# Layer-normalisation scaling moved from VectorE to GpSimd, and a residual sum cut in four, in an attention kernel

## What is computed

```python
x = x + 0.5 * ffn(layernorm(x))
x = x + attn(layernorm(x))
x = x + 0.5 * ffn(layernorm(x))
```

## Time and profile before

| | us |
|---|---|
| median of 3 executions | 3069.32 |
| lowest and highest | 3068.89, 3074.65 |
| the profiled execution, its own time | 3079.44 |
| its span, first to last instruction | 3077.6 |
| mean granted TensorE clock | 0.973 |

### The profile page before, as it was taken

The page is one execution under the profiler, slowest core; times in us unless marked ns, Lnnn a source line. Parts: engine busy times, 40 slices in busy tenths (PEclk is TensorE's granted clock), DMA queues, the critical chain, the costliest instruction groups (busy, mean ns, idle before and its releaser), DMA issues.

```text
span 3077.6 us, 96889 instructions
## 1 busy us (share of the span) xinstructions
PE 2752.8 (89%) x36160; PEld 1078.5 (35%) x36160; DVE 2810.2 (91%) x5659; ACT 2737.8 (89%) x5028; POOL 899.5 (29%) x1195
## 2 busy tenths in 40 slices
PE   5989998989989899898998988988988888898887
PEld 2323443434434334343343433333323333232323
DVE  4999999999999999999999998999999999899986
ACT  2999888988889888898888989898998989899897
POOL 3333213322133221332313332122332312233222
PEclk8999999999999999999999999999999999999999
DMA  8222342323423234232341323433223343322332
GB/s 221 53 48 60 57 98 40 68 49 56 98 38 63 55 56 98 37 62 57 56 98 36 61 59 70 85 70 63 50 59 69 70 85 64 67 48 61 72 70 56
DMA packets 155355, 206.63 MB, mean 67 GB/s; under 512 B 34530, under 2 KB 88290, under 8 KB 154723
## 3 DMA queue, kind: packets, MB, share of 16 engines
q1 hardware_dynamic: 154594, 199.37, 31.3%
q0 software_dynamic: 256, 0.52, 0.1%
HBM read 46.66 MB, written 25.17 MB: 23 GB/s over the span
## 4 chain that ended last, share of the span: by engine, by line
PE 36%; issue 20%; SPq 18%; DVE 11%; POOL 8%; ACT 4%; DMA 2%; DVEq 0%; POOLq 0%; ACTq 0%
SPq L374 18%; PE ring L833 12%; PE ring L770 11%; PE o_acc L847 10%; DVE exp_ring L656 9%; POOL kq_parts L365 2%; POOL kq_rest L361 2%; POOL kq_parts L363 2%; POOL kq_parts L359 2%; PE ring L892 1%; ACT exp_ring L580 1%; DMA kq_stack<-kq_parts 1%; POOL v_scaled L513 1%; ACT w_xn L592 1%; PE ring L869 1%
## 5 line engine op out<-in xcount | busy, mean ns | idle before, releaser
L580 ACT ACTIVATE exp_ring<-exp_ring,neg_max 128x1024 f32<-128x1024 f32 x2048 | 2344.7, 1146 | 271.3 <-DVE exp_ring L656 254.5
L656 DVE TENSOR_SCALAR_CACHE_REDUCE exp_ring<-ring 128x1024 f32<-128x1024 f32 x2048 | 2408.9, 1216 | 189.1 <-PE ring L833 184.5
L833 PE MATMUL ring<-kq_stack 128*32 128x512 bf16 x16384 | 1165.7, 387 | 201.2 <-DVE exp_ring L656 50.7
L847 PE MATMUL o_acc<-exp_ring,v_scaled 128*32 128x512 f32 x8224 | 1091.7, 607 | 59.1 <-POOL v_scaled L513 37.9
L833 PEld LDWEIGHTS ring<-kq_stack 128*32 128x32 bf16 x16384 | 401.9, 97 | 1147.2 <-issue 413.3
L513 POOL TENSOR_TENSOR v_scaled<-v_now,exp_rsums 128x64 f32<-128x64 f32 x513 | 155.2, 303 | 1790.1 <-DVE exp_rsums L671 1770.4
L580 ACT ACTIVATION_READ_ACCUMULATOR exp_ring<-exp_ring,neg_max 128x1 f32 x2048 | 381.9, 186 | 0.0
L847 PEld LDWEIGHTS o_acc<-exp_ring,v_scaled 128*32 128x32 f32 x8224 | 249.7, 112 | 293.8 <-POOL v_scaled L513 64.4
L770 PE MATMUL ring<-ffn_wo_wowff,o_T 128*32 128x256 f32 x4352 | 258.4, 380 | 4.2 <-DVE exp_ring L656 2.8
L770 PE MATMUL ring<-xn_T,ffn_wqkv 128*32 128x512 f32 x2112 | 257.8, 609 | 3.0 <-DVE exp_ring L656 1.9
L359 POOL TENSOR_TENSOR kq_parts<-kq_stage,zero 128x512 bf16<-128x512 f32 x130 | 143.0, 1100 | 225.7 <-ACT kq_stage L610 144.5
(11 more groups left out here) (102 smaller groups left out, 1283.0 us busy)
## 6 DMA issues: line engine op xcount, KB each, us to landing
kq_stack<-kq_parts SPq DMA_DIRECT2D x2072, 64.0 KB, 2.4
x_post<-x_slots SPq DMA_DIRECT2D x17, 1024.0 KB, 5.5
x_prep<-x_slots SPq DMA_DIRECT2D x16, 1024.0 KB, 8.3
x_slots<-x_post SPq DMA_DIRECT2D x8, 1024.0 KB, 6.1
out<-x_post SPq DMA_DIRECT2D x8, 1024.0 KB, 4.5
x_prep<-in_L_attn_x SPq DMA_DIRECT2D x1, 1024.0 KB, 6.0
exp_ring<-in_L_attn_w_qkv SPq DMA_DIRECT2D x1, 512.0 KB
kq_stack<-kq_parts POOLq DMA_DIRECT2D x8, 64.0 KB, 3.6
```

Of the source, the lines that this page charges most:

```text
L580: nc.scalar.activation(e, e, ACT.Exp, bias=negmax[:, i % NM:i % NM + 1], scale=-1.0, accum_out=sums[:, g % EG, c:c + 1]).then_inc(exp_done, 1)
L656: nc.vector.tensor_scalar(E[:, (g % EG) * HQ + c, :].rearrange("p (b n) -> p b n", b=NB), ps, -1.0, None, ALU.mult, ALU.min, accum_out=neg ...
L833: last = mm(ps[k:k + COLS, n, :], kq[:, 0, c, j * P + k:j * P + k + COLS], kq[:, 1, c, n * BANK:(n + 1) * BANK], start=True, stop=True)
L847: last = mm(O[32 * c:32 * c + 32, n, :], vsc[a][:, g % EG, c, :], E[:, (g % EG) * HQ + c, n * BANK:(n + 1) * BANK], start=(a == 0 and j == ...
```

## The change

Both normalisations' scaling goes from VectorE to GpSimd. On GpSimd it is a `tensor_scalar` with two operands, add and multiply, so the mean is negated first, once per normalisation, in a small operation behind the power. Ahead of the first call, and of any call that directly follows a split in GpSimd's order, stands a one-element addition into `pool_sink`. The places of `xn` and `xn2` stay. `x1` has four pieces of two token tiles, a tile apart, and the places of `ln2_stats` follow them. The waits on `x1_done` count to four.

```diff
+    X1 = 4
+    POOL_STEPS = ("ln_rstd", "ln2_rstd", "xn", "xn2", "qk", "recip", "u_norm", "w_norm", "xbias")
...
     PLAIN = {
-        "x1": (72.1, 72.2),
+        "x1": (72.1, 73.1, 74.1, 75.1),
...
     WITH_LINEAR = {
-        "x1": (36.1, 36.2),
-        "ln2_stats": (36.3, 36.7, 36.8, 36.8, 38.2, 38.4, 38.6, 39.1),
+        "x1": (35.1, 36.1, 37.1, 38.1),
+        "ln2_stats": (36.2, 37.2, 37.4, 38.2, 38.4, 39.2, 39.4, 40.1),
...
     SP:
-                    sp.wait_ge(x1_done, (p + 1) * 2)
+                    sp.wait_ge(x1_done, (p + 1) * X1)
                     sp.dma_start(tokens(out[p - LINEAR]), xr[:]).then_inc(out_stored, 16)
...
     GpSimd, in part():
+                    if kind in POOL_STEPS:
+                        after_split, prev = prev == "qk", kind
                     if kind == "ln_rstd":
                         pool.wait_ge(var_ready, p + 2)
                         nc.gpsimd.tensor_tensor(rstd[:], rstd[:], half_neg[:], ALU.pow).then_inc(rstd_ready, 1)
+                        nc.gpsimd.tensor_tensor(negm[:], zero[:, 0:1].to_broadcast([P, NT]), mv[:, :, 0],
+                                                ALU.subtract).then_inc(negm_ready, 1)
+                    elif kind == "xn":
+                        if i == 0:
+                            pool.wait_ge(negm_ready, p + 2)
+                            pool.wait_ge(rstd_ready, p + 2)
+                        if i == 0 or after_split:
+                            nc.gpsimd.tensor_tensor(psink[:], zero[:], zero[:], ALU.add)
+                        nc.gpsimd.tensor_scalar(xp[:, i, :], xp[:, i, :], negm[:, i:i + 1], rstd[:, i:i + 1],
+                                                ALU.add, ALU.mult).then_inc(xn_ready, 1)
...
+                    elif kind == "xn2":
+                        if i == 0:
+                            pool.wait_ge(negm2_ready, p + 1)
+                            pool.wait_ge(rstd2_ready, p + 1)
+                        if i == 0 or after_split:
+                            nc.gpsimd.tensor_tensor(psink[:], zero[:], zero[:], ALU.add)
+                        nc.gpsimd.tensor_scalar(wb[:, i, 0:D], xr[:, i, :], negm2[:, i:i + 1], rstd2[:, i:i + 1],
+                                                ALU.add, ALU.mult).then_inc(xn2_ready, 1)
...
     VectorE, in part():
-                        k = NT // 2
+                        k = NT // X1
...
-                    elif kind == "xn":
-                        dve.wait_ge(rstd_ready, p + 2)
-                        nc.vector.tensor_scalar(xp[:, i, :], xp[:, i, :], mv[:, i, 0:1], rstd[:, i:i + 1],
-                                                ALU.subtract, ALU.mult).then_inc(xn_ready, 1)
...
-                        dve.wait_ge(x1_done, p * 2 + i // 4 + 1)
+                        dve.wait_ge(x1_done, p * X1 + i // (NT // X1) + 1)
...
-                    elif kind == "xn2":
-                        dve.wait_ge(rstd2_ready, p + 1)
-                        nc.vector.tensor_scalar(wb[:, i, 0:D], xr[:, i, :], mv2[:, i, 0:1], rstd2[:, i:i + 1],
-                                                ALU.subtract, ALU.mult).then_inc(xn2_ready, 1)
```

More of the change, by code:

```diff
@@ L205, in build_macaron @@
         rstd2 = sb("rstd2", [P, NT])
+        negm = sb("neg_mean", [P, NT])
+        negm2 = sb("neg_mean2", [P, NT])
+        psink = sb("pool_sink", [P, 1])
         ssu = sb("sumsq_u", [P, NT])
@@ L273, in build_macaron @@
         xn2_ready = sem("xn2_ready")
+        negm_ready = sem("negm_ready")
+        negm2_ready = sem("negm2_ready")
         xt2_act = sem("xt2_act")
@@ L291, in build_macaron @@
                          y_dve: 4, xbias_done: 4, x_stored: 16, ln2_stats: NT, ln2_aggr: NT,
-                         var2_ready: 1, rstd2_ready: 1, xn2_ready: NT}
+                         var2_ready: 1, rstd2_ready: 1, xn2_ready: NT, negm2_ready: 1}
         START = 2
@@ L433, in phase @@
                 if isinstance(p, int):
-                    sp.wait_ge(x1_done, 2)
+                    sp.wait_ge(x1_done, X1)
                 elif not linear:
-                    sp.wait_ge(x1_done, (p + 1) * 2)
+                    sp.wait_ge(x1_done, (p + 1) * X1)
                     sp.dma_start(tokens(out[p - LINEAR]), xr[:]).then_inc(out_stored, 16)
@@ L453, in _ @@
             sp.dma_start(xr[:], tokens(xs[PHASES - 1])).then_inc(xr_loaded, 16)
-            sp.wait_ge(x1_done, (PHASES + 1) * 2)
+            sp.wait_ge(x1_done, (PHASES + 1) * X1)
             sp.dma_start(tokens(out[B - 1]), xr[:]).then_inc(out_stored, 16)
@@ L476, in part @@
             def part(steps, p, linear):
-                rank = ranks(steps)
+                rank, prev = ranks(steps), ""
                 for step in steps:
                     kind, i, r = step[0], index(step), rank[step]
+                    if kind in POOL_STEPS:
+                        after_split, prev = prev == "qk", kind
                     if kind == "ln_rstd":
@@ L486, in part @@
                         nc.gpsimd.tensor_tensor(rstd2[:], rstd2[:], half_neg[:], ALU.pow).then_inc(rstd2_ready, 1)
+                        nc.gpsimd.tensor_tensor(negm2[:], zero[:, 0:1].to_broadcast([P, NT]), mv2[:, :, 0],
+                                                ALU.subtract).then_inc(negm2_ready, 1)
+                    elif kind == "xn2":
[6 more added lines that the diff above has]
+                                                ALU.add, ALU.mult).then_inc(xn2_ready, 1)
                     elif kind == "qk":
@@ L535, in part @@
                         pool.wait_ge(bias_dve, START + p + 1)
-                        pool.wait_ge(x1_done, (p + 1) * 2)
+                        pool.wait_ge(x1_done, (p + 1) * X1)
                         nc.gpsimd.tensor_tensor(
```

## The result

The change takes **3101.5 us** (median of 4 runs, 3097.8 to 3108.4) against 3069.1 for the kernel before on the same chip: ratio 1.0104 [1.0088, 1.0119], slower by 32 us. I had forecast 3058, with a range of 3040 to 3085. The time lies above the range, and the sign was missed too.

What follows compares the result with a forecast made beforehand. No single engine was taken as the bound: VectorE, ScalarE and TensorE hand tiles on through three PSUM slots. Linear -3.6, plain -8.8, prologue +1.8 and end -0.6 sum to -11.2 us, giving a median of 3058, range 3040 to 3085.

Steps and rivals of the forecast that it cites:

- Plain phase, -8.8 us: Eight plain phases: moving xn off VectorE gains 1.1 of the possible 1.3 us a phase, -8.8 us in all.
- full from there: Plain phase: after the 1.69 us pair of xn goes, with ScalarE's 1.11 us wait behind it, ScalarE has no idle time.
- four tiles on: Plain phase: TensorE asks for group 10's scaling at place 49.1, so about 1.65 us of delay was taken to meet slack.
- x1 in pieces, 0: Four pieces of x1: some 0.2 us a phase more on VectorE, covered by ScalarE or other waits, so 0 net.
- Linear phase, -3.6: Eight linear phases: GpSimd's chain worked in order brings the gram 0.45 us earlier a phase, -3.6 us in all.
- c = 0.50: Time of one moved tensor_scalar call on GpSimd, start to start: 0.50 us, range 0.31 to 0.70.
- Prologue +1.8: Prologue: TensorE waits for all eight xn, 4.0 us on GpSimd plus 0.45 against 2.67 on VectorE, so +1.8 us.
- End -0.6: End of the kernel: the last x1 covers two token tiles in place of four, 1.23 us becoming about 0.65, -0.6 us.
- GpSimd becomes the bound: Rival at the linear phases' splits, places 34 to 53: calls of 0.66 us make the kernel slower, 3081 us; chance 0.28.
- c = 0.58: Time per GpSimd call from which the slower rival decides: 11.2 us over 144 calls and more on the path.
- The signs I had named: TensorE waiting 1 to 2 us at group 8, gram near 25.7 us, plain tiles 30 to 60 near 38.2, prologue about 2 later.

Runs made afterwards that it cites:

- experiment 4: The change with xn at other places, behind the fourth split in plain phases and ahead of place 34.2 in linear ones: 3068.2 us, ratio 1.0001 to the kernel before.
- experiment 7: The change with the third and fourth splits of the plain phases three tiles earlier, at 34.2 and 38.7: 3083.6 us, ratio 1.0043 to the kernel before.
- experiment 1: The kernel before with only the change's four pieces of x1 and places of ln2_stats, both scalings on VectorE: 3079.1 us against 3070.1, ratio 1.004.
- experiment 5: The change with x1's four pieces together at 36.1 to 36.25 and ln2_stats at the places of before: 3088.6 us, ratio 1.0066 to the kernel before.
- experiment 2: The change with xn2 put back on VectorE, so xn alone on GpSimd: 3105.4 us, ratio 1.0117 to the kernel before.
- experiment 3: The change with xn put back on VectorE, so xn2 alone on GpSimd: 3066.7 us, ratio 0.999 to the kernel before.
- experiment 8: The change with xn at other places, x1's pieces together and the plain phases' third and fourth splits earlier: 3058.9 us, ratio 0.9959 to the kernel before.
- experiment 9: The kernel before with only the third and fourth splits of the plain phases at 34.2 and 38.7: 3090.9 us, ratio 1.0059.

## Why the prediction was wrong

- **Plain phase, -8.8 us: the step that failed.** I took ScalarE to be "full from there" and stopped at tile 60. The gain of 1.04 a phase is there in the window that I read (tiles 30 to 60 take 38.26 us in the change, where I had said 38.2); then tile 64 waits for SP's 32 transfers behind the fourth split, and returns it and 1.5 more: 12.3 us for the eight phases in place of -8.8. The rows were at hand: SP's queue was 18% of the chain, and I asked of SP only what x_post and the result would do. Of the moved xn 3, 4 and 5 I priced the delay of the scaling of group 10 ("four tiles on"), and not that of the split, whose consumer is 22 tiles on and has none to spare. Experiments 4 and 7 show this cause: the wait shrinks or goes as the fourth split ends earlier.
- **x1 in pieces, 0: wrong.** It costs 9 us alone (experiment 1) and 13 in the change (experiment 5). I said that what it frees waits too; I didn't ask what a piece at 38.1 and statistics up to 40.1 push back. That VectorE has maxima waiting at those tiles, where the burst of before fell in a pause, is only argued; experiments 1 and 5 show that the places do most of it. The piece was mis-sized as well: 0.15 us each is fixed, where I took 0.1.
- **Linear phase, -3.6: sign wrong, order right.** In the phase that I worked the gram comes 0.53 later, not 0.45 earlier. Of that 1.0 us, 0.6 is what stands on GpSimd ahead of it. The first six calls take 3.23 for 3.0, the sink beside x1 0.53 for 0.15, and the split ahead of both 5.17 for 4.97 (its third part takes 1.51 for 1.04, beside another piece of x1); 0.4 of this is taken up again before the calls of xn2, which add 0.2. The other 0.4 is that TensorE takes the gram 0.49 us after the last scaling, behind a product that it is in, where I had allowed 0.1. I had also worked one of the longer phases: its gram stood 25.7 us behind the split, the mean of the eight was 25.3 and is 26.3 now. That makes 0.95 us a phase, the 7.7 us of tiles 28 to 53. Experiments 1 to 3 give the parts there: x1 +4.7, xn +11.0, xn2 -9.2. Of the remaining 4.8 of the 12.5 us, 3.3 are the granted clock in tiles 0 to 4, and 1.5 have no cause shown.
- **c = 0.50: right to a tenth, by luck.** It is 0.54 to 0.55, made of other parts: 0.35 us fixed and 0.80 ns per element, where I took 0.10 and the affine_select's 1.54; the two errors nearly cancel at 256 elements. The slope is close to the memset's 0.84. The Trainium skill (GPSIMD Engine Reference, Engine selection) calls one-input work roughly line rate there; in the slope the traces agree, if VectorE's x1 is the measure (685 ns for 512 elements and 1218 for 1024, 1.04 ns each), and the fixed part makes a call of 256 elements still 1.6 times VectorE's 0.33.
- **Prologue +1.8: +2.3**; 4.30 us for eight calls, with mean and sink 0.46. **End -0.6: -0.55.** Both held.
- **The rivals.** "GpSimd becomes the bound" had the right side and, with 3081, the nearer number, but its deciding point c = 0.58 wasn't reached: at 0.55 the kernel is slower by more than it gave for 0.70. It was not the price of a call that made the bound but what stands behind the calls. The signs I had named showed half of this: TensorE's wait at group 8 came, and the plain windows of tiles 30 to 60 came too, which could not show tile 64.

GpSimd's timeline and TensorE's answer in the prologue:

```profile
15.88 4.30 POOL L501 TENSOR_SCALAR x_prep<-x_prep,neg_mean,rstd 128x256 f32<-128x256 f32 x8
...
20.33 3.00 PE L890 MATMUL ring<-identity,x_prep 128*128 128x128 f32 x13 [20.33 <-POOL x_prep L501]
```

The parts, as profiled: linear +12.5, plain tiles 32 to 64 +12.3, prologue +2.3, end -0.5, the other plain stretches -8, in all 18.4. The medians are 14 further apart, which is how the two profiled executions stand in their runs.

## What to carry to other kernels

Before a step is moved to another engine, list what is queued behind it there, down to the DMAs, and follow each to its consumer and its due time, however many tiles on; a queue that is on the chain of waits has no slack, even where its engine is idle two thirds of the time. Give the moved step new places: here the move, with x1 in pieces, costs 1% at its old places, and with new ones, for it, for x1 and for the splits around it, the kernel is 0.4 to 0.8% faster than before. What new places would give with the scalings left on VectorE was not run. And read windows to the next point where everything has to meet, since a gain inside a window may be paid back just behind it.

## What was not expected of the hardware

- A GpSimd tensor_scalar with two per-partition operands takes 0.35 us + 0.80 ns per element, worked out from two sizes (553 ns at 256, 451 ns at 128), so halving its columns saves a fifth.
- The same call took up to 2.09 us beside VectorE's x1 (experiment 8):

```profile
L501 POOL TENSOR_SCALAR x_prep<-x_prep,neg_mean,rstd x136: 547/553/2087, 16.0 to 2927.2; 128x256 f32<-128x256 f32 x136
```

  In the phase shown above it started 0.07 us after x1 did and ended 0.26 us after the third of x1's four pieces; the fourth piece took 0.88 us where the others took 0.69, and GpSimd's next call 0.98. The Trainium skill (SBUF — State Buffer, SBUF: two separate sides) has the two engines share one pair of ports, as an exclusive lock held for a whole instruction, when VectorE reads two inputs from SBUF and GpSimd reads SBUF too; x1 and the scaling do, and the trace agrees that one waits for the other. It also shows three pieces of x1 in a row go ahead of the waiting call, which that sentence leaves open. In the change itself no call of the scaling lies beside x1, and the longest of them was 562 ns; there it is the sink that meets a piece (0.53 us for 0.19).
- Contention is not lifted by moving the victim: VectorE's xn beside GpSimd's splits cost 669 ns on average (experiment 9), GpSimd's beside VectorE's x1 668 (experiment 8, 89.4 us for 136 calls, of which 16 are slow and the others near 553). It is the places that have to differ.
- TensorE's clock is part of the price of a wait. Behind the waits at tile 64 of the change (2.4 to 3.6 us) it stood at 1.2 GHz in five of eight phases (0.63 us for a product of 512 columns in place of 0.38); behind those of before (at most 1.5 us) in none. The length of the wait does not decide it alone: in experiment 4 it was slow behind waits of 1.9 and 2.5 us and not behind one of 2.4.
- SP took 0.69 us for each of these transfers of 64 KB (64 in 44 us in both kernels; in experiment 8 it took 46.9 us for 64). 32 of them and the landing of the last are a latency of about 24 us.
